# A routed expert layer on one core: token slots of the first four expert pairs computed ahead of the others, and four weight loads with other start conditions

## What is computed

```
x   = x + gnn(xn) + mix(xn)
h   = layernorm(x)                                   # 1250 x 512
logits = einsum('td,hde->hte', h, hash_proj)         # 4 hashes, 64 experts
cand = argmax(logits, -1); scores = max              # one candidate of each hash
sel  = the candidates of the 2 best scores           # 1250 x 2 experts
for each expert e:                                   # buffers of up to 156 rows
    y[rows of e] = gelu(h[rows of e] @ W1[e]) @ W2[e]
x   = x + mean of the two expert outputs of each row
```

## Time and profile before

| what | value |
|---|---|
| median of three executions | 561.43 us (560.75 to 561.58) |
| the profiled execution, its own time | 566.19 us |
| its span, first to last instruction | 564.4 us |
| TensorE matmul busy | 531.3 us, 94% |
| VectorE, ScalarE, GpSimd busy | 347.1, 248.6, 94.1 us |
| routing from `pick` to the first transpose of a pair | 379.21 to 396.05 us |
| experts, tr 0 to the last `down` | 396.05 to 546.2 us |

### The profile page before, as it was taken

One profiled execution on the slowest core, in us unless ns is written; L12 is line 12 of the kernel. 1 busy time (PEld: TensorE's weight loads), 2 busy tenths in 40 slices (PEclk: granted clock), 3 DMA queues, 4 the chain that ended last, 5 costly groups with the idle time before them and its releaser, 6 DMA issues.

```text
span 564.4 us, 8447 instructions
## 1 busy us (share of the span) xinstructions
PE 531.3 (94%) x2791; PEld 367.6 (65%) x2793; DVE 347.1 (62%) x973; ACT 248.6 (44%) x534; POOL 94.1 (17%) x119
## 2 busy tenths in 40 slices
PE   0799999999999999999999999999799999999997
PEld 0344444455478888899999999986455544555445
DVE  3888787776875545638887233497254444454767
ACT  1787766676544543135665222442343433333300
POOL 4141101100000000000000000003244444445300
PEclk9999999999998999999999999999899999999999
DMA  8500000000020006474007222987999999999977
GB/s 299 205 2 1 1 1 1 1 1 0 2 76 0 1 0 215 160 254 185 2 0 319 93 74 86 401 337 262 325 353 415 417 416 409 417 415 416 369 278 284
DMA packets 32409, 105.69 MB, mean 187 GB/s; under 512 B 4640, under 2 KB 10017, under 8 KB 25324
## 3 DMA queue, kind: packets, MB, share of 16 engines
q1 hardware_dynamic: 22364, 86.09, 39.6%
q10 hardware_dynamic: 5120, 9.25, 4.7%
q0 software_dynamic: 4880, 9.78, 4.6%
HBM read 93.48 MB, written 17.84 MB: 197 GB/s over the span
## 4 chain that ended last, share of the span: by engine, by line
PE 72%; DVE 10%; DMA 8%; issue 6%; POOL 1%; ACT 1%; DVEq 1%; SPq 0%; POOLq 0%; ACTq 0%
PE PS L527 8%; PE PS L526 8%; PE PS L528 8%; PE PS L601 6%; PE PS L564 5%; PE PS L556 5%; PE PS L824 4%; PE PS L810 4%; PE PS L630 4%; DMA BIG<-xx_rows,TIDX 4%; PE PS L631 4%; DMA XG<-xx_rows,TIDX 3%; PE PS L747 3%; PE PS L590 3%; DMA XA<-in_x 1%
## 5 line engine op out<-in xcount | busy, mean ns | idle before, releaser
L526 PE MATMUL PS<-ROUND 128*128 128x416 f32 (+3 forms) x232 | 83.9, 361 | 0.0
L527 PE MATMUL PS<-ROUND 128*128 128x416 f32 (+3 forms) x232 | 83.6, 360 | 0.0
L528 PE MATMUL PS<-ROUND 128*128 128x416 f32 (+3 forms) x232 | 83.4, 359 | 0.0
L824 PE MATMUL PS<-BIG 128*64 128x512 f32 x208 | 53.0, 593 | 1.3 <-DVE BIG L1219 1.3
L1061 DVE BATCH_NORM_STATS2 BST<-BIG 128x6 f32<-128x416 f32 (+1 forms) x36 | 20.7, 590 | 44.2 <-ACT BIG L1397 35.6
L630 PE MATMUL PS<-ROUND 128*128 128x416 f32 (+3 forms) x120 | 44.5, 371 | 2.3 <-DVE ROUND L978 1.8
L960 DVE TENSOR_TENSOR BIG<-PS,BIG 128x280 f32 (+17 forms) x69 | 30.7, 444 | 23.8 <-PE PS L590 19.9
L526 PEld LDWEIGHTS PS<-ROUND 128*128 128x128 f32 (+1 forms) x232 | 43.5, 188 | 2.6
L528 PEld LDWEIGHTS PS<-ROUND 128*128 128x128 f32 (+1 forms) x232 | 43.6, 188 | 2.5
L527 PEld LDWEIGHTS PS<-ROUND 128*128 128x128 f32 (+1 forms) x232 | 43.5, 188 | 2.4
L631 PE MATMUL PS<-ROUND 128*128 128x416 f32 (+3 forms) x120 | 43.2, 360 | 0.0
(11 more groups left out here) (258 smaller groups left out, 970.2 us busy)
## 6 DMA issues: line engine op xcount, KB each, us to landing
BIG<-in_we SPq DMA_DIRECT2D x46, 1024.0 KB
BIG<-in_we SPq DMA_DIRECT2D x12, 512.0 KB
y_rows<-KVB SPq DMA_DIRECT2D x19, 256.0 KB
BIG<-y_rows SPq DMA_DIRECT2D x9, 512.0 KB, 7.3
EXTRA<-in_we SPq DMA_DIRECT2D x4, 1024.0 KB
XA<-in_we SPq DMA_DIRECT2D x4, 1024.0 KB
BIG<-in_wqkvp ACTq DMA_DIRECT2D x3, 1024.0 KB, 14.9
XA<-in_we SPq DMA_DIRECT2D x6, 512.0 KB
```

Source lines behind the costliest of these rows:

```text
L526: mm(o, ah, bh, start=first, stop=False)
L527: mm(o, ah, bl, start=False, stop=False)
L528: return mm(o, al, bh, start=False, stop=last)
L824: ins = mm(PS[64 * j:64 * j + 64, b, :], HT[:, s, 128 * f2 + 64 * j:128 * f2 + 64 * j + 64], weights(2 * r + j, 1024 + 512 * f2, 512), sta ...
```

## The change

Three things, all around the routing.

1. The slots of experts 0 to 7 (`NEAR` = 8, four pairs) get a small copy of the whole chain: `OHE0` (20 x 8 entries instead of 20 x 64), `OHS0`, the counts `near` on TensorE (10 products), `PRD0`, `RAW0`, `QP0`, `LQ0`, `OHV0` on GpSimd, `slots0` (40 products of 4 columns), and the first four columns of `TIDX`. GpSimd gathers pairs 0 to 3 from them and waits for the rest of `TIDX` only before pair 4.
2. The chain for all 64 experts follows behind. Its `OHE` is made in two halves between steps of the small chain. Its `OHV` moves from GpSimd (2 instructions) to ScalarE (20 instructions of 64 elements). Its `slots` and `most` move on TensorE to just ahead of up 1, and its `TIDX`, `SCIDX` and `most` on VectorE (`far_tokens`) behind `root(0)`. `FILL` falls from 22 to 10, `idle` from 7 + 11 to 8 + 8.
3. On SP, experts 18 and 22 wait for the last two `xx_rows` tiles and for `slots0`, no more for the first gather; 19 waits for `slots`.

```diff
-FILL = 22
+FILL = 10
+NEAR = 8
+SLOTS_BEFORE = ("up", 1)
...
             pe.wait_ge(s_pool, 3)
+            b, use = bank("near")
+            idle(b, 8)
+            pe.wait_ge(s_ohs, 2)
+            mm(PS[:, b, 0:NEAR * NT], TRIB[:, :], OHS0, start=True, stop=False)
+            for q in range(1, NT):
+                ins = mm(PS[:, b, NEAR * q:NEAR * NT], ONEB[:, :], OHS0[:, 0:NT - q, :], start=False, stop=(q == NT - 1))
+            ins.then_inc(full[b], 1)
+            b, use = bank("slots0")
+            idle(b, 8)
+            pe.wait_ge(s_par, 2)
...
             b, use = bank("below0")
-            idle(b, 7)
-            pe.wait_ge(s_ohs, 2)
+            pe.wait_ge(s_ohs, 3)
...
+                if step == SLOTS_BEFORE:
+                    far_slots()
...
-                V.tensor_tensor(OHS, OHE[:, :, 0, :], OHE[:, :, 1, :], ALU.add).then_inc(s_ohs, 1)
+                V.tensor_tensor(OHS0, OHE0[:, :, 0, :], OHE0[:, :, 1, :], ALU.add).then_inc(s_ohs, 1)
+                one_hots(0, 5)
...
             root(0)
+            far_tokens()
...
             A.activation(FIRST, EPS[:, 0:1], ACT.Gelu)
+            for a in range(20):
+                act.wait_ge(s_sel, 3 + a // 10)
+                ins = A.activation(OHV[:, a, :, :], OHE[:, a // 2, a % 2, :].rearrange("p (r j) -> p j r", j=2), ACT.Identity,
+                                   scale=CST[:, 702 + a:703 + a])
+            ins.then_inc(s_ohv, 1)
...
-            pool.wait_ge(s_tidx, 1)
+            b, use = at_of("slots0")
+            pool.wait_ge(moved[b], use)
             for g, (i, e) in enumerate(GROUPS):
                 pool.wait_ge(sd_xx[g], 16 * (e - i))
-            b, use = at_of("slots")
-            pool.wait_ge(full[b], use)
-            for r in range(LEAD):
+            for r in range(NEAR // 2):
+                gather_pair(r)
+            pool.wait_ge(s_tidx, 1)
+            for r in range(NEAR // 2, LEAD):
                 gather_pair(r)
...
-            for q in range(2):
-                sp.wait_ge(sd_xx[q], 64)
-                load_expert(16 + q)
-            sp.wait_ge(sd_xg[0], 16)
-            for e in (18, 19, 22):
-                if e == 22:
-                    sp.wait_ge(sd_xx[2], 32)
-                load_expert(e)
+            b, use = at_of("slots0")
+            for q, (i, e) in enumerate(GROUPS):
+                sp.wait_ge(sd_xx[q], 16 * (e - i))
+                if q == 2:
+                    sp.wait_ge(full[b], use)
+                    load_expert(18)
+                load_expert((16, 17, 22)[q])
+            b, use = at_of("slots")
+            sp.wait_ge(full[b], use)
+            load_expert(19)
```

More of the change, by code:

```diff
@@ L227, in bank_plan @@
         nb += 1
-    for key in ("below0", "below1", "slots", "most"):
-        fill(key, nb % 8)
-        nb += 1
+    for key, b in (("near", 4), ("slots0", 5), ("below0", 6), ("below1", 7), ("slots", 5), ("most", 4)):
+        fill(key, b)
     for step in expert_order():
@@ L413, in gnn_mix_moe @@
         EQB = scr(768).bitcast(BF16).rearrange("p (a e) -> p a e", e=NEXP)
[L414 to L418, removed]
+        OHE0 = RT[:, 0:10 * NEAR].bitcast(BF16).rearrange("p (i k e) -> p i k e", i=NT, k=2)
+        OHS0 = RT[:, 80:80 + 5 * NEAR].bitcast(BF16).rearrange("p (i e) -> p i e", i=NT)
+        PRD0 = RT[:, 120:120 + 20 * NEAR].rearrange("p (i k e) -> p i k e", i=NT, k=2)
+        RAW0, QP0 = RT[:, 280:300], RT[:, 300:310].bitcast(F16)
+        OHV0 = RT[:, 310:310 + 10 * NEAR].bitcast(F16).rearrange("p (a j r) -> p a j r", a=20, j=2)
+        LQ0 = RT[:, 390:1030].bitcast(F16).rearrange("p (a q) -> p a q", a=20)
+        OHE = RT[:, 2048:2688].bitcast(BF16).rearrange("p (i k e) -> p i k e", i=NT, k=2)
+        PRD = RT[:, 2688:3968].rearrange("p (i k e) -> p i k e", i=NT, k=2)
+        LQ = RT[:, 2688:3328].bitcast(F16).rearrange("p (a q) -> p a q", a=20)
+        OHV = RT[:, 3968:4608].bitcast(F16).rearrange("p (a j r) -> p a j r", a=20, j=2)
+        LESS, SECOND = big(4608, 32), big(4640, 32)
         XG = [TM2[:, 0, :], TM2[:, 1, :], TM2[:, 2, :], XG4[:, :], KSUM[:, :], RB[:, 0:512], RB[:, 512:1024], big(4608, D)]
@@ L762, in tensor @@
             pe.wait_ge(s_pool, 3)
+            b, use = bank("near")
[8 more added lines that the diff above has]
+            pe.wait_ge(s_par, 2)
+            for j in range(20):
+                if j in (0, 14):
+                    pe.wait_ge(s_lq, 1 + j // 14)
+                for h in range(2):
+                    ins = mm(PS[64 * h:64 * h + 64, b, 0:NEAR // 2], LQ0[:, j, :], OHV0[:, j, h, :], start=(j == 0),
+                             stop=(j == 19))
+            ins.then_inc(full[b], 1)
             b, use = bank("below0")
-            idle(b, 7)
-            pe.wait_ge(s_ohs, 2)
+            pe.wait_ge(s_ohs, 3)
             mm(PS[:, b, 0:512], TRIB[:, :], OHS[:, 0:8, :], start=True, stop=False)
@@ L774, in tensor @@
             mm(PS[:, b, 64:128], ONEB[:, :], OHS[:, 0, :], start=False, stop=True).then_inc(full[b], 1)
[L775 to L788, removed]
+            b, use = at_of("near")
             pe.wait_ge(moved[b], use)
@@ L791, in tensor, with far_slots @@
                 mm(PS[:, b, 0:512], TRIB[:, :], OHS[:, 0:8, :], start=True, stop=True)
+            def far_slots():
+                b, use = bank("slots")
+                pe.wait_ge(s_ohv, 1)
+                for j in range(20):
+                    if j in (0, 14):
+                        pe.wait_ge(s_lq, 3 + j // 14)
+                    for h in range(2):
+                        ins = mm(PS[64 * h:64 * h + 64, b, 0:32], LQ[:, j, :], OHV[:, j, h, :], start=(j == 0), stop=(j == 19))
+                ins.then_inc(full[b], 1)
+                b, use = bank("most")
+                pe.wait_ge(s_most, 1)
+                transpose(PS[0:1, b, 0:128], EST[:, 3:4], IDN).then_inc(full[b], 1)
             for step in ro:
@@ L1166, in vector @@
                     pick()
+            b, use = at_of("near")
+            dve.wait_ge(full[b], use)
+            V.tensor_tensor(PRD0, OHE0, PS[:, b, 0:NEAR * NT].rearrange("p (i e) -> p i e", e=NEAR).unsqueeze(2).broadcast_to(
+                [128, NT, 2, NEAR]), ALU.mult).then_inc(moved[b], 1)
+            dve.wait_ge(moved[b], use)
+            link(V.tensor_reduce(RAW0.unsqueeze(2), PRD0.rearrange("p i k e -> p (i k) e"), AX.X, ALU.add))
+            link(V.tensor_tensor(QP0, RAW0, SAME, ALU.add))
+            positions(LQ0, QP0)
+            one_hots(5, NT)
+            b, use = at_of("slots0")
+            dve.wait_ge(full[b], use)
+            tokens(b, NEAR // 2, LESS)
+            V.scalar_tensor_tensor(TIDX[:, 0:NEAR // 2], PS[:, b, 0:NEAR // 2], float(N), LESS[:, 0:NEAR // 2], ALU.add,
+                                   ALU.min).then_inc(moved[b], 1)
+            dve.wait_ge(s_sel, 4)
+            V.tensor_tensor(OHS, OHE[:, :, 0, :], OHE[:, :, 1, :], ALU.add).then_inc(s_ohs, 1)
             for q, (i, e) in enumerate(((0, 8), (8, NT))):
@@ L1176, in vector, with far_tokens @@
             link(V.tensor_tensor(QP, RAW, SAME, ALU.add))
[L1177 to L1179 removed]
+            positions(LQ, QP)
             link(V.tensor_tensor(POSf, RAW, SAME, ALU.add))
             V.tensor_reduce(EST[:, 3:4], POSf, AX.X, ALU.max).then_inc(s_most, 1)
[L1182 to L1193 removed]
+            def far_tokens():
+                b, use = at_of("slots")
+                far = slice(NEAR // 2, 32)
+                dve.wait_ge(full[b], use)
+                tokens(b, 32, LESS)
+                V.scalar_tensor_tensor(TIDX[:, far], PS[:, b, far], float(N), LESS[:, far], ALU.add, ALU.min).then_inc(s_tidx, 1)
+                link(V.tensor_scalar(SECOND, PS[:, b, 0:32], 0.0, None, ALU.is_lt))
+                dve.wait_ge(moved[at_of("slots0")[0]], at_of("slots0")[1])
+                dve.wait_ge(s_tidx, 1)
+                V.scalar_tensor_tensor(SCIDX[:, :], TIDX[:, :], 2.0, SECOND, ALU.mult, ALU.add).then_inc(moved[b], 1)
+                b, use = at_of("most")
+                dve.wait_ge(full[b], use)
+                V.tensor_reduce(FLAG[0:1, 1:2], PS[0:1, b, 0:128], AX.X, ALU.max).then_inc(moved[b], 1)
+                dve.wait_ge(moved[b], use)
+                V.tensor_copy(FLAGI[0:1, 1:2], FLAG[0:1, 1:2]).then_inc(s_res, 1)
             def root(p):
```

24 lines of the change are left out of this document (18 added, 6 removed).

## The result

The changed kernel takes 565.41 us, the median of six executions (564.13 to 569.61); six of the kernel before beside them took 561.5 us (560.45 to 562.86). The ratio is 1.0082, 95% interval 1.0059 to 1.0104: **slower by 0.8%, 4 to 5 us**, where 2.5 us less were predicted.

A forecast was written before the change was run, and what follows sets the result against it. The expert part was taken as bound by TensorE's train of products, not by weights, so moving `up 2` moves nearly all behind it. An `up 2` gain of 2.7 us, counted as 2.5, gave 561.43 - 2.5 = 558.9 us, range 556.8 to 561.9.

The forecast's parts named there:

- The gather's landing: First gather, ahead of the experts: bounds 392.4 to 397.6, tr 0 forecast at 394.4, 1.6 us earlier.
- Nearest is the third one: First gather priced like the third, issued as expert 18's load began: packets 4.0 us after issue, 1.0 us to move.
- When it goes out: First gather's issue on GpSimd: at 389.3 instead of 392.63, 3.3 us earlier, held by the `xx_rows` writes.
- a difference counts the same in both: Whole sum: reckoned in the profiled execution's time, 566.19 us, 4.8 above the median of 561.43.
- hole of 2.14 us: TensorE without a product ahead of `up 1`: `slots` and `most`, 0.74 + 0.2 us, were to partly fill it.
- `up 2` at 406.6: Expert part on TensorE: `up 2` starts there instead of 409.33, 2.7 us earlier; 2.5 us counted as gained.
- From tr 0 to `up 2`: Start of the experts on TensorE: 10.1 us at full clock plus 2.1 us of lower clock, 12.2 us.
- No `up` waits for a weight: Expert train on TensorE: weights run some 4 us or more ahead, so no `up` stands idle for one.
- the early loads: Experts 18 and 22 on SP: their earlier start is worth nothing by itself.
- the tail: After the experts: `y_rows` reads have 2.0 us to spare, so up to 3.5 us of gain pass through.
- The slower one: Rival: loads of 17, 18, 22 ahead of gather 0, 8.3 us; tr 0 at 397.6; 562.4 us, chance 0.14.
- the cheaper gather: Rival: gather 0 waits only for expert 17's remainder; tr 0 at 392.5, clock stays up; 557.2 us, chance 0.20.

The follow-up runs named there:

- before_again: The kernel before, unedited, run and profiled once more: 561.07 us, ratio 1.0009; profiled execution 561.16 us.
- before_w_early: The kernel before with only experts 18 and 22 loaded ahead of the first gather, nothing of the small chain: 567.23 us, ratio 1.0076.
- fill36_again: The changed kernel with FILL = 36 instead of 10, measured again beside the changed kernel on one chip: 563.47 us, ratio 1.0044.

## Why the prediction was wrong

**The gather's landing, the step that failed.** The prediction had bounds of 3.1 and 8.3 us for it and chose "Nearest is the third one": 389.3 + 4.0 + 1.0. Measured: 8.0 us from the issue to tr 0, close to the upper bound. The third gather was a bad neighbour: it was issued 0.3 us ahead of expert 18's load, gather 0 now goes out 1 us behind it. So the row does not show, as the prediction says of it, a gather that passed 2 MB queued ahead: that load went out behind it. What stands ahead on SP's queue when the gather goes out separates 3.4 from 8.0, and the prediction read only how much traffic there would be. For the same reason it took no account of which of the two engines gets past their common wait first.

**When it goes out.** Predicted 389.3, 7.6 us behind `SEL`; measured 8.91. The bound was the right one (`xx_rows`, not `TIDX`). Its landing was 0.4 us later than assumed (387.62 is 7.93 behind `SEL`), and the 0.9 us that GpSimd takes from its release to the issue, which the prediction had added to `TIDX`, it left out for `xx_rows` but for 0.1. Together tr 0 is 4.2 us later than forecast (16.89 behind `SEL`, not 12.7): 1.3 from the issue, 3 from the landing.

**The yardstick.** "a difference counts the same in both" is the second failed step. The profiled execution of before had a hole of 2.14 us, where the repeat stands 0.72, and 1.7 us of lower clock that the repeat doesn't have: `up 2` at 27.64 behind `SEL` there, 24.54 in the repeat. The prediction itself noted that the execution was 4.8 us above the median and that the trace didn't explain the hole, and still counted on filling it. About half of the 4.8 us was not even in this part: `SEL` itself began 2.4 us later than in the repeat. Its `up 2` at 406.6 is 24.9 behind `SEL`. Had everything gone as forecast, the gain against the repeated execution would have been below nothing, -0.4 us. The small chain is worth 24.54 - 22.80 = 1.7 us at `up 2`, and about 2 us in the time. In sum, at `up 2` a gain of 2.7 was forecast and 4.7 were lost; of these 7.5 us, 4.2 are the later tr 0, 0.2 the way from it to `up 2`, and 3.1 the yardstick.

**What was right.** From tr 0 to `up 2` 12.2 us were forecast and 12.4 measured, the lower clock on tr 0 and `up 0` as forecast. The small chain was done in time, though later than forecast: `TIDX` is ready 7.15 us behind `SEL`'s start (386.84 and 379.69), not 5.5 to 6.5, and still 0.8 us ahead of the last `xx_rows` write. No `up` waits for a weight, so the early loads are worth nothing. The train runs at 129.4 / 29 = 4.46 us a pair (4.49 forecast), and the tail passes all on.

**The rivals.** The slower one had the mechanism word for word (loads ahead of gather 0, 8.3 us, nearly 6 us without a product, lower clock), deciding from tr 0 later than 396.9, which is 15.2 behind `SEL`; measured 16.89. It gave 562.4 and not 565.4, for it was reckoned against the unusual execution: `up 2` "1.0 us later than now" would have been 4.1 later than in the repeat. It had a chance of only 0.14, for the rule that was quoted for the cheaper gather and for the third gather's row.

The rule, from the Trainium skill, "DMA: Bandwidth & Descriptors", section "Queues, rings and completion order", says that each DMA engine goes round between the queues with work and changes after a whole packet. The runs don't bear out what I drew from it. Under it I expected the gather's packets and the weights' to alternate, but in 392 to 394 us 18 of the one stand against 115 of the other, and 1 MB queued ahead costs 3.3 to 3.8 us. (What the profile counts as a packet need not be a packet of the rule.) The landings of the changed kernel are near the order of issue:

```profile
BIG<-in_we SPq DMA_DIRECT2D x1, 1024.0 KB, 6.9
BIG<-in_we SPq DMA_DIRECT2D x1, 384.0 KB, 8.6
XA<-in_we SPq DMA_DIRECT2D x1, 512.0 KB, 10.9
```

Expert 18, issued at 387.63, has landed at 394.5; gather 0, issued at 388.60, at 396.4; the first part of 22, issued at 388.00, at 396.6; its second, also ahead of the gather, at about 398; its last, issued at 388.96, at 399.9. So a first-come order of the two queues is not excluded either. Whether the time goes into the packets' turns or into making the gather's descriptors beside those of the weights, no run here separates.

**Open.** The hole behind `up 0` in the first profile of before: it was seen in none of the 13 later profiles, of which only two (before_again and before_w_early) have the kernel before's order of products there, and what held ScalarE up there isn't known. How the 4.6 us of the gather's delay come about below the level of packets, and what makes the clock fall around 172 us in some executions, is not known either.

## What to carry to other kernels

A small transfer that an engine stands waiting for must go out ahead of the bulk loads that nobody waits for; if both hang on the same event on two queues, make the bulk wait for the small one, as whichever engine issues first otherwise decides. Before counting on a hole in a trace, look whether the execution it comes from is a usual one, and where it is longer than the others: here one that was 0.9% over the median held 2.4 us ahead of the part under study and a hole in it, and its repeat neither. And a later start has its clock cost on top, in the two profiles of the changed kernel 2 and 5 us on 4.5 us of delay.

## What the runs showed of the hardware

- Two engines released by the same transfer don't issue together: SP's load goes out 0.01 us after the landing (387.62, 387.63), GpSimd's gather 0.98 us after it (388.60), without a wait for anything else between.
- A gather of 128 rows (issue to tr 0) took 3.25 to 3.9 us when the nearest 1-MB load was issued 2 us or more ahead of it, 6.65 and 7.2 when one was issued within the last 1 us, and 7.2 (before_w_early), 7.9, 8.0 (the two profiles of the changed kernel) and 8.6 (fill36_again) with two, the last 512 KB of the second behind it.
- After about 5.4 us without a product the granted clock was 0.50, and it stayed low, counted from the start of tr 0, for about 5 us in one execution and about 11 in another (to the end of `up 1` at 407.6; 0.67 in 406 to 408). With idle times of 1.13 and 0.72 us it fell in one execution and held in another (0.91 and 0.72 us).
